# Moving two shared down products behind the last experts, turning the first slots sooner, summing one tile's ranks on GpSimd

## The reference

```python
h = _layernorm(x) * (1 + ca) + sa
x = x + ga * attention(h)                       # one head, causal, residual inside
h = _layernorm(x) * (1 + cb) + sb
# FFN: sigmoid gate over 32 experts in 4 groups, top 2 groups, top 4 experts of each token
h1  = silu(einsum('ech,ehf->ecf', buf, w1)) * einsum('ech,ehf->ecf', buf, w3)
ob  = einsum('ecf,efh->ech', h1, w2)            # 32 experts x 64 slots
out = (y.reshape(n, K, H) * topk_w[:, :, None]).sum(1)
shared = silu(x @ shared_gate) * (x @ shared_up) @ shared_down
x = x + gb * (out + shared)
```

## Time and profile before

| | us |
|---|---|
| median of 3 runs | 153.12 |
| the three runs | 152.9, 153.12, 154.01 |
| span of the profiled execution | 152.4 |
| device time of the profiled execution | 154.15 |
| busy in the span: PE | 144.8 (95%) |
| busy: DVE | 110.8 (73%) |
| busy: ACT | 63.0 (41%) |
| busy: POOL | 47.3 (31%) |

### The profile page before, as it was taken

The page is one execution under the profiler, slowest core; times in us unless marked ns, Lnnn a source line. Parts: engine busy times, 40 slices in busy tenths (PEclk is TensorE's granted clock), DMA queues, the critical chain, the costliest instruction groups (busy, mean ns, idle before and its releaser), DMA issues.

```text
span 152.4 us, 2722 instructions
## 1 busy us (share of the span) xinstructions
PE 144.8 (95%) x895; PEld 106.8 (70%) x895; DVE 110.8 (73%) x390; ACT 63.0 (41%) x168; POOL 47.3 (31%) x68
## 2 busy tenths in 40 slices
PE   7979799999999999999999999999999999999792
PEld 7846457958666677589888878875666665688681
DVE  2758999787998649779975992436778778257984
ACT  3134771277243542974995981012434331100000
POOL 7500003429913000000000003777777776500000
PEclk9999999999999999999999999999999999999999
DMA  3999999999999999600200300445542211159993
GB/s 99 294 378 351 419 417 392 353 348 348 348 350 351 349 348 349 224 5 0 77 0 0 120 0 2 118 116 118 110 120 60 86 64 50 63 157 364 410 327 120
DMA packets 21904, 31.27 MB, mean 205 GB/s; under 512 B 2017, under 2 KB 17927, under 8 KB 21890
## 3 DMA queue, kind: packets, MB, share of 16 engines
q1 hardware_dynamic: 20498, 27.71, 53.1%
q0 software_dynamic: 1392, 3.39, 8.8%
HBM read 23.65 MB, written 8.13 MB: 208 GB/s over the span
## 4 chain that ended last, share of the span: by engine, by line
PE 66%; DMA 12%; DVE 11%; SPq 3%; issue 3%; ACT 2%; POOL 1%; DVEq 0%; POOLq 0%
PE bank L1569 9%; PE bank L1377 7%; PE score_pair L1234 7%; PE bank L1234 6%; DMA w_sb<-results 6%; PE score_pair L1429 6%; PE score_pair L1355 5%; PE score_pair L1351 5%; DMA w_sb<-in_L_wmod_dram 4%; PE bank L1429 4%; PE bank L1591 3%; PE bank L1364 3%; PE score_pair L1553 2%; PE score_pair L1377 2%; SPq L403 2%
## 5 line engine op out<-in xcount | busy, mean ns | idle before, releaser
L467 POOL DMA_INDIRECT arena<-token_rows,gather_idx x16 | 16.4, 1022 | 49.0 <-DVE gather_idx L1000 44.4
L1569 PE MATMUL bank<-w_sb,arena 128*64 128x256 f32 x128 | 17.0, 387 | 0.0
L1377 PE MATMUL bank<-arena 128*128 128x256 f32 x56 | 13.7, 381 | 0.0
L450 POOL TENSOR_TENSOR base<-aT,mod 128x256 f32<-128x256 f32 x8 | 5.9, 734 | 24.3 <-DVE aT L813 19.6
L476 POOL DMA_INDIRECT results<-arena,res_idx x11 | 11.1, 1005 | 3.9 <-issue 2.4
L1569 PEld LDWEIGHTS bank<-w_sb,arena 128*64 128x64 f32 x128 | 8.3, 136 | 5.2 <-issue 2.0
L1377 PEld LDWEIGHTS bank<-arena 128*128 128x128 f32 x56 | 10.2, 190 | 1.8 <-issue 0.5
L561 ACT ACTIVATE prob<-score_pair,nmax 128x128 f32<-128x128 f32 (+7 forms) x8 | 5.9, 743 | 11.6 <-DVE nmax L884 11.6
L1355 PE MATMUL score_pair<-arena 128*128 128x512 f32 (+3 forms) x24 | 10.2, 504 | 0.0
L1351 PE MATMUL score_pair<-arena 128*128 128x512 f32 (+3 forms) x24 | 9.8, 490 | 0.0
L1591 PE MATMUL bank<-w_sb,prob 128*64 128x256 f32 x64 | 8.3, 381 | 0.0
(11 more groups left out here) (208 smaller groups left out, 333.3 us busy)
## 6 DMA issues: line engine op xcount, KB each, us to landing
w_sb<-in_L_ffn_w_dram SPq DMA_DIRECT2D x12, 1024.0 KB, 12.5
results<-prob SPq DMA_DIRECT2D x1, 4096.0 KB, 15.0
w_sb<-results SPq DMA_DIRECT2D x6, 512.0 KB, 8.3
token_rows<-rows SPq DMA_DIRECT2D x8, 144.0 KB
xin<-in_L_attn_x_dram SPq DMA_DIRECT2D x4, 256.0 KB, 6.2
w_sb<-in_L_wmod_dram SPq DMA_DIRECT2D x1, 1024.0 KB, 9.4
w_sb<-results SPq DMA_DIRECT2D x4, 256.0 KB, 6.6
out_dram<-base SPq DMA_DIRECT2D x8, 128.0 KB, 2.7
```

The source lines that it names most:

```text
L467: nc.gpsimd.indirect_dma_start(out=slot_in[:, r, :], out_offset=None, in_=rows_d, in_offset=bass.IndirectOffsetOnAxis(ap=gather_idx[:, r:r ...
L1377: last = t.matmul(PV_BANK[i][:, 0:H], probT[:, i % 2, j, :], vo[:, j, :], start=(j == 0), stop=(j == i))
L1569: last = t.matmul(bank[4 + g % 2][CAP * side:CAP * side + CAP, 2 * F * r:2 * F * r + 2 * F], slotT[:, k, CAP * e:CAP * e + CAP], w13_sb[:, ...
```

## The change

1. `shared_down(1)` no longer stands ahead of `turn_slots(0)`; its two parts take the places that the parts of `shared_down(2)` had (one ahead of the first expert products, one after them). DVE's `shared_add(1)` moves behind `slot_evac(1)`, ahead of `expert_hid(0)`.
2. `shared_down(2)` moves behind the last `expert_down`, ahead of the first `return_first`; it writes bank 1 where it wrote bank 3. DVE's `shared_add(2)` moves behind `shared_add(3)`. `turn_hid(1)` loses its wait for `base_done`.
3. Tile 4 joins `ON_DVE`: PE no longer multiplies its ranks with the identity. POOL adds them instead, by two additions behind its last scatter, when `yin[4]` has landed; DVE adds that sum to `base` by one new instruction (`add_pool_ranks(4)`), behind `add_sums(4)`.
4. The sum banks are dealt out anew, and PE makes the sum of tile 5 ready behind the wait for `base_done` 4 together with tile 7's.

```diff
-        SHD_BANK = [bank[b] for b in (6, 2, 3, 0)]
+        SHD_BANK = [bank[b] for b in (6, 2, 1, 0)]
+        SHD_ORDER = [0, 1, 3, 2]
...
-        ON_DVE = (0, 1, 2, 3, 6)
-        SUM_BANK = [bank[(i + 1) % NT] for i in range(NT)]
+        ON_DVE = (0, 1, 2, 3, 4, 6)
+        SUM_BANK = [bank[b] for b in (2, 4, 3, 5, 7, 1, 6, 0)]
...
+            y = yin[4]
+            pool.wait_ge(y_loaded[4], 16)
+            nc.gpsimd.tensor_tensor(y[:, 0:2 * H], y[:, 0:2 * H], y[:, 2 * H:4 * H], ALU.add).then_inc(ranks_added, 1)
+            pool.wait_ge(ranks_added, 1)
+            nc.gpsimd.tensor_tensor(y[:, 0:H], y[:, 0:H], y[:, H:2 * H], ALU.add).then_inc(ranks_added, 1)
...
             def shared_add(j):
-                dve.wait_ge(shd_mm, j + 1)
+                dve.wait_ge(shd_mm, SHD_ORDER.index(j) + 1)
...
             slot_evac(0)
-            shared_add(1)
             for g in range(EGROUPS - 1):
                 slot_evac(g + 1)
+                if g == 0:
+                    shared_add(1)
                 expert_hid(g)
                 scores_of_slots(g)
                 if g == 0:
-                    shared_add(2)
                     score_sums()
...
             shared_add(3)
+            shared_add(2)
...
+            def add_pool_ranks(i):
+
+                dve.wait_ge(ranks_added, 2)
+                v.scalar_tensor_tensor(out=base[:, i, :], in0=yin[i][:, 0:H], scalar=scale2[:, i:i + 1],
+                                       in1=base[:, i, :], op0=ALU.mult, op1=ALU.add).then_inc(final_done, 1)
...
             add_sums(4)
+            add_pool_ranks(4)
             add_ranks(6)
...
                 if g >= 2:
                     pe.wait_ge(hidT_done, g - 1)
-                else:
-                    pe.wait_ge(base_done, 2 + g)
+                elif g == 0:
+                    pe.wait_ge(base_done, 2)
...
-            shared_down(1)
             turn_slots(0)
-            shared_down(2, (0,))
+            shared_down(1, (0,))
...
                 if g >= 1:
                     expert_down(g - 1)
                 else:
-                    shared_down(2, (1,))
+                    shared_down(1, (1,))
...
             expert_down(last_g)
+            shared_down(2)
...
-            for i in (6, 4, 5):
+            for i in (6, 4):
                 return_first(i)
                 return_last(i)
             pe.wait_ge(base_done, NB)
-            return_first(7)
-            return_last(7)
-            add_ranks(4)
+            for i in (5, 7):
+                return_first(i)
+                return_last(i)
             add_ranks(5)
             add_ranks(7, 1)
```

More of the change, by code:

```diff
@@ L293, in adaln_attention_moe @@
         final_done = sem("final_done")
+        ranks_added = sem("ranks_added")
         def ring_plan():
```

## The result

| | kernel before | changed kernel |
|---|---|---|
| median of 6 runs each, us | 153.78 | 156.98 |
| lowest to highest, us | 152.9 to 154.38 | 156.25 to 157.4 |
| span of the profiled execution, us | 152.4 | 155.3 |
| busy in the span, PE | 144.8 (95%) | 142.6 (92%) |
| busy, DVE | 110.8 (73%) | 113.0 (73%) |

The changed kernel takes 1.0198 of the time before, 95% interval 1.016 to 1.0236: 2.0% slower. Between the two profiled executions the last sum on DVE starts 2.91 us later (149.70 to 152.61) and the span ends 2.9 us later, so the whole difference is in what leads to DVE's last sum. The granted TensorE clock is not part of it: the page of the changed kernel shows it at full speed in all slices but the last, which lies behind PE's last product.

What follows compares the result with a forecast made beforehand. The prediction took DVE's unbroken run from tile 3's sum, started by PE, as the bound. Later sums 1.13, DVE's own work 0.02 and POOL beside DVE 1.9 made 3.05 us on the median 153.12: 156.2 us, range 154.0 to 157.0.

Steps and rivals of the forecast that it cites:

- What bounds the end: Tail: DVE runs unbroken from tile 3's sum with 0.49 us of slack; PE's start of the sums decides, not the loads.
- The advance of the loop: Expert loop: with `shared_down(1)` gone from ahead of `turn_slots(0)`, that starts 0.80 us sooner and the loop 0.6 us sooner.
- the loss at `turn_hid(0)`: Start of the expert loop: PE waits for `expert_hid(0)`, now behind `shared_add(1)`, and loses 0.2 to 0.25 us.
- The loads: POOL's scatter can begin 0.58 us sooner, and SP's loads of `results` start and land 0.6 us sooner.
- `shared_down(2)` uncovered: Between the last `expert_down` and the first sum on PE: its four matmuls add 1.73 us that nothing covers.
- The sums later by 1.13 us: Tile 3's sum on DVE starts at 139.76 instead of 138.63: 1.73 us of product less 0.60 of advance.
- DVE's own work: DVE's tail: `add_pool_ranks(4)` adds 0.51 us, 0.49 us of slack vanish, together +0.02 us.
- POOL beside DVE: DVE's ranks in the tail: POOL's two additions, 2.0 us in all, hold DVE for 1.9 us.
- The rule weighed against the row: DVE's ranks beside POOL: loss 1.9 us if held for whole instructions, 1.0 if 0.5 us for each addition.
- The port costs DVE little: Rival for DVE's tail beside POOL: 1.15 us of loss left, 154.3 us, up to 155.4; chance 0.24.
- The loads are the bound: Rival for the tail: loads of `results` start 0.6 us sooner and the end moves with them, 152.5 us; chance 0.07.
- POOL is the last: Rival for the tail: POOL's second addition ends near 149 and DVE waits about 1 us for it, 157.2 us; chance 0.07.

Runs made afterwards that it cites:

- the moves alone: Changed kernel with tile 4's ranks back on PE and no POOL or DVE additions for them; 1.0171 and 1.0183 of the kernel before.
- the two spare additions: Kernel before plus two POOL additions beside DVE's ranks, written to a spare place nobody reads; 1.0067 of the kernel before.
- POOL's part alone: Kernel before with tile 4's ranks added by POOL and one more DVE instruction, no shared product moved; 1.0075 and 1.0109 of the kernel before.
- the kernel without the wait: Changed kernel with `turn_slots(0)` no longer waiting for DVE's `shared_add(0)`; 1.0141 and 1.0211 of the kernel before.
- tile 4 on DVE: Changed kernel with tile 4's two rank additions made by DVE instead of POOL; 1.017 and 1.0246 of the kernel before.

## Why the prediction was right, point by point

It forecast 156.2 us and 2.0% slower; the ratio is 1.0198. The forecast difference of 3.05 us is 2.9 between the spans and 3.2 between the medians. The mechanism was right. That the sum comes so close is partly luck: one term was 0.26 too small and another 0.4 too big. The time is at the edge, too: it was added up from a median of 153.12, the six runs of the kernel before have 153.78, and 156.98 lies just inside the range that ended at 157.0 and just outside the 155.5 to 156.9 of the forecast itself. By its steps:

- **What bounds the end.** Right. DVE runs from tile 3's sum without a pause, and its slack was 0.50 by the moves alone, against 0.49 read from spacings.
- **The advance of the loop, 0.6 us.** Right in sign, too big: `turn_slots(0)` came 0.59 us sooner relative to `shared_down(0)` (3.46 to 2.87), not 0.80, and after the loss at `turn_hid(0)` 0.39 were left (the last expert product is 0.33 sooner on the clock of the span, which starts its shared products 0.06 later). What was wrong is the way from DVE's end to PE's start, taken as 0.04: DVE ended at 99.27 and PE started at 99.53. The signal itself was right. In the event records of PE's queue the wait for `base_done` is over at 99.31, 0.04 behind DVE's end; behind it stands one more wait instruction, at 99.42, and then the weight load at 99.50. The forecast had put these at nothing. The loss at `turn_hid(0)`, 0.2, was right, cause and size: `expert_hid(0)` ran from 105.34 behind `shared_add(1)`, and PE followed at 105.81.
- **The loads.** Right in sign, too big: the scatter came 0.26 us sooner, not 0.58, and SP's first load 0.27, not 0.6 (133.51 to 133.24). It made no difference, since DVE came to `yin[6]` late.
- **`shared_down(2)` uncovered, 1.73 us.** Right: 1.72.
- **The sums later by 1.13 us.** 1.39 by the span (138.63 to 140.02), by the error of the advance.
- **DVE's own work, +0.02 us.** Right: 0.52 for L1219 with its spacing, 0.50 of slack used.
- **POOL beside DVE, 1.9 us.** Right in mechanism, 0.4 too much: L1203 lost 0.97 and L1201 0.53, together 1.50. I took nearly the whole of POOL's 2.0 us. A DVE instruction that is caught loses less than POOL's instruction lasts (0.97 of 1.26, 0.53 of 0.79): it starts 0.09 and 0.13 us behind POOL's, and it ends only 0.28 and 0.55 us behind POOL's end where it usually takes 0.48 and 0.68, so part of its own time overlaps. Over all traces with additions on POOL the loss was between 0.9 and 1.5 us. The errors of this term and of the sums' start, -0.4 and +0.26, cancel in part.
- **The rule weighed against the row.** By "no more than 0.5 us for each" the loss would have been 1.0, by whole instructions 1.9; it was 1.5. Wide instructions lose with the length of POOL's, and not entirely. The Trainium skill, "SBUF — State Buffer", section "Who interferes with whom", calls the shared pair of ports an exclusive lock and says "for the whole instruction" in its point on DVE's 2-port modes; of two SBUF inputs it says that they contend with GpSimd's reads. The prediction took the first for the second too, and the traces bear that out in part: 1.50 us lost of 2.05.
- **The rivals.** "The port costs DVE little" falls by the changed kernel's stretched rows and by the two spare additions. (Its upper end, 155.4, was added up wrong: 1.15 and half of 1.9 on 153.12 are 155.2.) "The loads are the bound" falls: SP's first load started 0.27 us sooner and the end came 2.9 later. "POOL is the last" did not occur: its second addition ended at 145.66, 4 us ahead of L1219.

## What to carry to other kernels

When every engine is nearly full, ask of a moved piece who stands behind it: a product put into PE's queue ahead of the first sum delays all of DVE's run (1.72 us, of which 1.39 were left after the loop's advance), and with the same product five microseconds further down the kernel takes the time of the kernel before. Work given to GpSimd beside a full VectorE is not free where GpSimd reads SBUF while VectorE's instructions have two SBUF inputs: it cost 0.9 to 1.5 us here, and in the changed order VectorE was 0.1 to 0.3 us sooner through when it did the two additions itself. Count slack from the spacings of instructions in a run and not from the chain of waits, which named the loads where DVE had 0.5 us to spare. And count the wait instructions that stand between a signal and the work: they, not the signal, made a fifth of a microsecond here.

## What the runs showed of the hardware that I had not expected

- Between DVE's end and PE's start there were 0.26 us, of which the signal took 0.04. The rest lies with the wait instructions of PE that stand behind: from 99.31 to the next at 99.42 and to the weight load at 99.50. With `shared_down(2)` behind tile 3's sum the same three steps take 0.04, 0.11 and 0.08 us.
- On chips 12, 2 and 9 the same kernel took 165 us where it took 154 on chip 13. The first 96 us agree within 3 us. In the three traces in which the shared products start latest (98.37, 98.46 and 99.12 us, against 96.03 to 97.10 in the others from these chips), the granted clock of TensorE was 0.81 to 0.86 of full speed on average from 16 to 20 us and 0.72 to 0.76 from 20 to 24, where all the others have 1.00. The expert loop differs more. From the start of `shared_down(0)` to the last `expert_evac` it takes 36.59 us in the kernel before, and 48.24 and 48.21 in POOL's part alone, which has the same order there. Engines stand for 2 to 4 us at a time on work that looks finished, as in this row of the kernel without the wait, where PE's transposes had ended at 103.62 by their row:

```profile
105.41 0.55 DVE L1118 TENSOR_SCALAR arena<-score_pair,modc 128x256 f32<-128x256 f32 x1 [3.68 <-remote]
```

  The semaphore that DVE waits for there was raised at 105.38, so DVE was not late; what held that signal for 1.8 us is open.

  The moves alone and tile 4 on DVE have the same instructions up to the end of that stretch, and took 49.55, 48.78, 46.59 and 47.20 us for it. So differences of 2 to 3 us in time on those chips can come from there, and the 1.7% of the moves alone can't be split further by these runs.
